# A four-block kernel on one core: the last block's two batch streams put half a period apart, its output projection and expert sums moved between engines

## The reference, cut to what matters

```python
x  = _layernorm(x_in)
n1 = _layernorm(x, ln1_w, ln1_b)
rw = _gating(n1, smha_sim, smha_gates)             # (1024, 8)
q = einsum('btc,ech,bte->bth', n1, q_proj, rw)     # k and v alike, 8 experts
attn = softmax(causal(q @ k.T * scale)) @ v        # (1024, 128)
attn_out = einsum('bth,ehc,bte->btc', attn, o_proj, rw)
hs = x + attn_out
n2 = _layernorm(hs, ln2_w, ln2_b)
rw2 = _gating(n2, moe_sim, moe_gates)
inter = gelu(einsum('btc,eci->btei', n2, w1))      # 8 experts
out = hs + einsum('btei,eic,bte->btc', inter, w2, rw2)
result = x_in + _layernorm(out)
```

## Time and profile before

| what | value |
|---|---|
| median of 3 runs | 3173.81 us (3173.39 to 3175.27) |
| the profiled execution, its own time | 3170.2 us |
| its span, first to last instruction | 3168.4 us |
| busy PE, PEld, DVE | 76%, 53%, 73% of the span |
| busy ACT, POOL | 53%, 40% of the span |
| mean granted TensorE clock | 0.866 |

### The profile page before, as it was taken

The page is one execution under the profiler, slowest core; times in us unless marked ns, Lnnn a source line. Parts: engine busy times, 40 slices in busy tenths (PEclk is TensorE's granted clock), DMA queues, the critical chain, the costliest instruction groups (busy, mean ns, idle before and its releaser), DMA issues.

```text
span 3168.4 us, 41094 instructions
## 1 busy us (share of the span) xinstructions
PE 2407.0 (76%) x14962; PEld 1690.2 (53%) x14962; DVE 2311.8 (73%) x4141; ACT 1678.5 (53%) x2552; POOL 1263.5 (40%) x1203
## 2 busy tenths in 40 slices
PE   3114776667676696899999999999999388667867
PEld 1002444344344564577777777776777366245635
DVE  3994798699599612688878878887888533874386
ACT  4223663665376242678777877787778124022402
POOL 0341143144124200365766576667667540114011
PEclk8556878888788898799999999999999789788978
DMA  3000000000000000100000100010000100000000
GB/s 99 0 0 0 0 1 1 1 1 1 1 1 1 1 1 14 41 21 21 24 21 21 28 21 21 24 29 21 21 21 1 40 1 1 0 14 1 1 0 14
DMA packets 32026, 41.96 MB, mean 13 GB/s; under 512 B 8897, under 2 KB 18130, under 8 KB 31442
## 3 DMA queue, kind: packets, MB, share of 16 engines
q1 hardware_dynamic: 31826, 39.34, 4.6%
HBM read 12.05 MB, written 2.10 MB: 4 GB/s over the span
## 4 chain that ended last, share of the span: by engine, by line
PE 46%; DVE 20%; issue 18%; POOL 11%; ACT 4%; SPq 1%; DMA 1%; POOLq 0%; DVEq 0%; ACTq 0%
PE ps L954 10%; PE ps L932 6%; PE ps L943 6%; POOL MA L379 5%; PE ps L710 3%; DVE MA L1090 3%; DVE MA L1410 3%; PE ps L914 2%; DVE lnb L265 2%; PE ps L1724 2%; PE ps L645 2%; PE ps L1711 2%; PE ps L647 1%; PE ps L646 1%; PE ps L1648 1%
## 5 line engine op out<-in xcount | busy, mean ns | idle before, releaser
L1090 DVE TENSOR_REDUCE MA<-ps 128x1 f32<-128x1024 f32 x512 | 623.1, 1220 | 190.4 <-PE ps L932 177.6
L379 POOL TENSOR_TENSOR MA<-MA,BIG 128x1024 f32<-128x1024 f32 x120 | 280.1, 2355 | 624.3 <-DVE BIG L350 624.3
L954 PE MATMUL ps<-MA,WB 128*64 128x128 f32 x4096 | 504.5, 277 | 0.0
L954 PEld LDWEIGHTS ps<-MA,WB 128*64 128x64 f32 x4096 | 442.8, 137 | 88.4 <-issue 87.4
L344 DVE TENSOR_TENSOR_SCAN BIG<-BIG 128x1024 f32<-128x1024 f32 x128 | 346.8, 2748 | 0.0
L932 PE MATMUL ps<-BIG 96*128 96x512 f16 x1024 | 312.6, 387 | 13.3 <-DMA BIG<-WB 4.9
L632 ACT ACTIVATE HR<-ps,b 128x512 f32<-128x512 f32 x288 | 191.5, 686 | 244.0 <-PE ps L647 243.0
L710 PEld LDWEIGHTS ps<-WB,HR 128*128 128x128 f32 x2304 | 305.8, 209 | 25.0 <-issue 8.7
L710 PE MATMUL ps<-WB,HR 128*128 128x128 f32 x2304 | 312.8, 294 | 0.0
L1017 ACT ACTIVATE WB<-ps,MA 128x1024 f32<-128x1024 f32 x206 | 229.5, 1114 | 149.3 <-DVE MA L1090 147.5
L497 PE MATMUL ps<-bc,sel 96*128 96x512 bf16 x256 | 108.2, 520 | 249.1 <-DVE BIG L350 190.7
(11 more groups left out here) (286 smaller groups left out, 5133.2 us busy)
## 6 DMA issues: line engine op xcount, KB each, us to landing
BIG<-BIG SPq DMA_DIRECT2D x192, 64.0 KB, 2.0
BIG<-WB SPq DMA_DIRECT2D x192, 64.0 KB, 2.0
WB<-w_dram SPq DMA_DIRECT2D x1, 2304.0 KB, 14.6
X<-x_dram SPq DMA_DIRECT2D x4, 512.0 KB, 12.5
HR<-w_dram SPq DMA_DIRECT2D x1, 2048.0 KB, 9.3
out_dram<-X SPq DMA_DIRECT2D x4, 512.0 KB, 3.2
WB<-wqkv_dram SPq DMA_DIRECT2D x1, 1536.0 KB, 6.1
WB<-w_dram SPq DMA_DIRECT2D x2, 512.0 KB, 8.2
```

Source lines behind the costliest of these rows:

```text
L379: e.tensor_tensor(yy[:, c, :], yy[:, c, :], db[n % 2][c], ALU.add).then_inc(*p_my.up(b, n, c))
L954: x = e.matmul(bank[6][64 * pp:64 * pp + 64, 0:128], V[(4 * b + g) % 2][:, k, 64 * pp:64 * pp + 64], DT[n % 2][:, 128 * k:128 * k + 128], ...
L1090: e.tensor_reduce(L_of(n)[:, c:c + 1], ps[s][:, :], AX, ALU.max, negate=True).then_inc(*v_amx.up(n, s))
```

## The change

The planned times get the stream in them: `d_at(k, r, t)` is `D_PERIOD * r + D_SHIFT * k + t` with a period of 193.0 and a shift of 96.0, so in each engine's order stream 1 stands half a period behind stream 0. The weight preparation becomes a generator that is merged with the two streams. The output projection treats each half of the rows and each expert by itself: POOL scales the attention rows (`n1`) by the expert's weight, PE transposes them, ACT copies them, and PE multiplies by that expert's matrix and sums the eight experts in PSUM (`B[h]`, a bank for each half); DVE adds each bank into `hs` once. In the expert phase DVE's four weigh-and-add operations become one 128x512 multiplication into `s_sc`, and POOL adds the result into `hs`. `affine` and the gate get further `yield`s. The removed transposes are those of `turn(r, 1)`.

```diff
-        D_PERIOD, D_EXPERT = 177.2, 3.15
-        D_LN = [(0, 3), (5, 8), (125.4, 128.4), (171.2, 174.2)]
-        D_TR = [11, 110, 131.4]
-        D_GATE = [(13, 16, 19, 21), (131.4, 134.4, 137.4, 139.4)]
+        D_PERIOD, D_EXPERT, D_SHIFT = 193.0, 3.15, 96.0
+        D_LN = [(0, 3), (5, 8), (139.5, 142.5), (187.5, 190.5)]
+        D_TR = [11, 110, 145.5]
+        D_GATE = [(13, 16, 19, 22), (145.5, 148.5, 151.5, 154.5)]
         D_ATT = [76.4 + 3.5 * i + 0.1 * i * (i - 1) for i in range(9)]
-        D_OUT, D_MOE = 111, 142.4
+        D_OUT, D_STEP, D_MOE, D_MSTEP = 111, 1.6, 157, 1.75
-        def d_at(r, t):
-            return D_PERIOD * r + t
+        def d_at(k, r, t):
+            return D_PERIOD * r + D_SHIFT * k + t
-        def d_scaled(r, q):
+        def d_scaled(k, r, q, more=0.0):
+            if q >= 16:
+                return d_at(k, r, D_OUT + D_STEP * (q - 16) - 1.5 + more)
...
         def experts_act(e):
-            e.wait_ge(phase, 8)
+            yield 0.3
...
+            yield 8.5
             e.wait_ge(s_wq, 16)
...
         def experts_dve(e):
-            e.wait_ge(phase, 8)
+            yield 0.2
...
             for a in range(3):
+                yield 13.2 + 3.5 * a
...
...
-                for j in range(8):
-                    yield d_at(r, D_OUT + 1.8 * (j + 1))
-                    e.wait_ge(*t_dom[k].at(r, j))
-                    for x in range(8):
-                        i = e.scalar_tensor_tensor(out=hs[:, j, :], in0=(S0, S1)[j % 2][:, 128 * x:128 * x + 128],
-                                                   scalar=G(6)[:, j, x:x + 1], in1=hs[:, j, :], op0=ALU.mult, op1=ALU.add)
...
+                for h in range(2):
+                    yield d_at(k, r, D_OUT + D_STEP * (8 * h + 9) + 1)
+                    e.wait_ge(*t_dom[k].at(r, 8 * h + 7))
+                    e.tensor_tensor(hs[:, 4 * h:4 * h + 4, :], hs[:, 4 * h:4 * h + 4, :],
+                                    B[h].rearrange("p (j c) -> p j c", c=128), ALU.add).then_inc(*v_dom[k].up(r, h))
...
-                    for j in range(4 * (x // 8), 4 * (x // 8) + 4):
-                        i = e.scalar_tensor_tensor(out=hs[:, j, :], in0=B[2 + x % 2][:, 128 * (j % 4):128 * (j % 4) + 128],
-                                                   scalar=G(6)[:, j, x % 8:x % 8 + 1], in1=hs[:, j, :], op0=ALU.mult,
-                                                   op1=ALU.add)
-                    i.then_inc(*v_dm[k].up(r, x))
+                    e.tensor_tensor(s_sc[k][x % 2].rearrange("p (j c) -> p j c", c=128),
+                                    B[2 + x % 2].rearrange("p (j c) -> p j c", c=128),
+                                    G(6)[:, 4 * h:4 * h + 4, x % 8:x % 8 + 1].to_broadcast([128, 4, 128]), ALU.mult).then_inc(
+                                    *v_dm[k].up(r, x))
...
-                    for q in range(16):
-                        h, x = q // 8, q % 8
-                        yield d_scaled(r, q)
+                    for q in range(32):
+                        h, x = q // 8 % 2, q % 8
+                        yield d_scaled(k, r, q)
...
+                for x in range(16):
+                    yield d_at(k, r, D_MOE + D_MSTEP * (x + 2) + 0.5)
+                    e.wait_ge(*v_dm[k].at(r, x))
+                    h = x // 8
+                    if x % 8:
+                        e.wait_ge(*p_dm[k].at(r, x - 1))
+                    e.tensor_tensor(s_hs[k][:, 4 * h:4 * h + 4, :], s_hs[k][:, 4 * h:4 * h + 4, :],
+                                    s_sc[k][x % 2].rearrange("p (j c) -> p j c", c=128), ALU.add).then_inc(*p_dm[k].up(r, x))
...
-                turned(r, 1)
+                for q in range(16, 32):
+                    yield d_scaled(k, r, q, 1.5)
...
+                    e.activation(s_so[k][q % 2], B[2 + q % 2], ACT.Copy, scale=1.0).then_inc(*a_dhi[k].up(r, q))
...
-                turn(r, 1)
-                for j in range(8):
-                    for h in range(2):
...
-                        i = e.matmul((S0, S1)[j % 2][:, 512 * h:512 * h + 512], xT[k][:, 128 * j:128 * j + 128],
-                                     flat(wo3[:, 4 * h:4 * h + 4, :]), start=True, stop=True)
+                for q in range(16, 33):
+                    if q < 32:
+                        yield d_scaled(k, r, q, 1.5)
+                        e.wait_ge(*p_dsc[k].at(r, q))
...
+                        for j in range(4):
+                            i = e.transpose(B[2 + q % 2][:, 128 * j:128 * j + 128], s_sc[k][q % 2][:, 128 * j:128 * j + 128],
+                                            ident[:, :])
+                        i.then_inc(*t_dst[k].up(r, q))
+                    if q > 16:
+                        y = q - 17
+                        h, x = y // 8, y % 8
+                        yield d_scaled(k, r, q, 2.0)
+                        e.wait_ge(*a_dhi[k].at(r, q - 1))
...
+                        for j in range(4):
+                            c = slice(128 * j, 128 * j + 128)
+                            i = e.matmul(B[h][:, c], s_so[k][y % 2][:, c], wo3[:, x, :], start=x == j == 0, stop=x == 7,
+                                         skip_group_check=True)
+                        i.then_inc(*t_dom[k].up(r, y))
...
-            experts_dve(e)
-            weave(soft_dve(e, 0), soft_dve(e, 1))
+            e.wait_ge(phase, 8)
+            weave(experts_dve(e), soft_dve(e, 0), soft_dve(e, 1))
```

More of the change, by code:

```diff
@@ L1243, in program @@
                 for k in range(2)]
+        s_so = [[big[4 + k][:, 512 * i:512 * i + 512] for i in range(2)] for k in range(2)]
         s_g = [big[7][:, 512 * k:512 * k + 512].rearrange("p (j n) -> p j n", j=8) for k in range(2)]
@@ L1288, in experts_pool @@
         def experts_pool(e):
-            e.wait_ge(phase, 8)
+            yield 6.0
             e.wait_ge(*a_dsp.at("sq"))
@@ L1336, in gating @@
                 top2(e, s_g[k], gidx[k], G(0), G(1), G(4), G(2), G(3)).then_inc(*dve_own.up())
+                ready = dve_own.now()
+                yield d_at(k, r, times[2] + 1.5)
                 e.tensor_scalar(G(7)[:, :, 4:5], G(1)[:, :, 0:1], 0.0, None, ALU.is_le)
                 e.tensor_scalar(G(7)[:, :, 5:6], G(1)[:, :, 0:1], 0.0, None, ALU.max)
-                e.wait_ge(*dve_own.now())
+                e.wait_ge(*ready)
                 e.tensor_tensor(G(2), G(2), G(3), ALU.add).then_inc(*dve_own.up())
@@ L1348, in gating @@
                     *v_dgt[k].up(r, w, "pre"))
-                yield d_at(r, times[3])
+                yield d_at(k, r, times[3])
                 e.wait_ge(*a_dtr[k].at(r, w, "exp"))
@@ L1373, in soft_dve @@
                     e.wait_ge(*t_dtr[k].at(r - 1, 2, 1))
-                affine(r, 1)
+                yield from affine(r, 1)
                 yield from gating(r, 0, D_GATE[0])
                 for q in range(16):
-                    yield d_scaled(r, q)
+                    yield d_scaled(k, r, q)
                     e.wait_ge(*a_dhi[k].at(r, q))
@@ L1419, in soft_dve @@
+                yield d_at(k, r, D_LN[2][0])
+                stats(e, s, hst, {0: v_dom[k].at(r, 0), 4: v_dom[k].at(r, 1)}).then_inc(*v_dln[k].up(r, 2, "stats"))
+                yield d_at(k, r, D_LN[2][1])
                 e.wait_ge(*p_dln[k].at(r, 2, "rstd"))
-                affine(r, 2)
+                yield from affine(r, 2)
                 yield from gating(r, 2, D_GATE[1])
                 for x in range(16):
-                    yield d_at(r, D_MOE + 1.6 * (x + 2))
+                    yield d_at(k, r, D_MOE + D_MSTEP * (x + 2))
@@ L1700, in soft_pe @@
+                yield d_at(k, r, D_TR[2])
                 turn(r, 2)
[L1701 removed]
+                yield d_at(k, r, D_GATE[1][2])
                 logits(r, 2)
@@ L1766, in _ @@
             e.drain().then_inc(phase, 1)
-            experts_act(e)
-            weave(soft_act(e, 0), soft_act(e, 1))
+            e.wait_ge(phase, 8)
+            weave(experts_act(e), soft_act(e, 0), soft_act(e, 1))
         @block.vector
@@ L1786, in _ @@
             e.drain().then_inc(phase, 1)
-            experts_pool(e)
-            weave(soft_pool(e, 0), soft_pool(e, 1))
+            e.wait_ge(phase, 8)
+            weave(experts_pool(e), soft_pool(e, 0), soft_pool(e, 1))
         @block.sync
```

178 lines of the change are left out of this document (86 added, 92 removed).

## The result

The changed kernel takes 3213.51 us (3213.22 to 3218.76, four runs), the kernel before 3173.6 beside it. The ratio is 1.0129, with an interval of 1.0111 to 1.0146: 40 us slower. The forecast was 3135, faster; the range ended at 3180.

A forecast was written before the change was run, and what follows sets the result against it. No engine bounds the whole stage; each phase has its own limit, and PE idles in norms. Lone start 87, three half periods of 147 and lone end 101 make 629 for 667.6, so 3135 us; range 3080 to 3180.

The forecast's parts named there:

- H = 112.6 + 34.5 = 147: Length in us of one half period of the last stage with both streams: PE work 112.6 plus waits 34.5.
- mixed half period: One of three half periods of the last stage in which both streams run, forecast at 147 us each.
- the two lone parts: Start and end of the last stage, where one stream runs alone: 87 and 101 us, sure to some 8 together.
- the 629: Forecast length in us of the last stage, 87 + 3 × 147 + 101, against 667.6 before.
- Lone start: Stream 0 alone at the stage's start: norms, gate, projection and five attention units, 87 us.
- Segments: Four stretches of a mixed half period, by stream 0's planned time 0, 24, 76, 88, 96: 38, 79, 22 and 8 us.
- Rival 1: In mixed half periods PE is nearly full, hiding the other stream's DVE and POOL: 127 us each, 3075 total; chance 0.20.
- Rival 2: POOL operations awaiting DVE hold up the other stream's scalings: half period 171 us, kernel slower at 3207; chance 0.12.
- Rival 3: ACT stands as long again at each table change, 11 us more a half period: 3168 us, about unchanged; chance 0.06.
- Rival 4: POOL's scalings slow DVE's norms, adding 5 us a half period (152): 3150 us, within the forecast; chance 0.14.

The follow-up runs named there:

- in step: The changed kernel with D_SHIFT 0 instead of 96.0, so both streams run in lockstep with the new operations: 3153.4 us, ratio to before 0.9927.
- the idle products: Unread 512-column PE products added to the changed kernel ahead of scores of units 5 to 7: 3228.88 us; to its D_SHIFT 0 version in the norms: 3156.66 us.

## Why the prediction was wrong

**The step that failed** is "H = 112.6 + 34.5 = 147". The two terms were right: 112.7 of work and 32 to 35 of waits. The sum was not, since a mixed half period held 20 to 23 us more, work at low clock and gaps, for which it had no term. Three times 20 is 60, and the two lone parts were 12.4 + 4.0 = 16 over. With these the 629 become 705; measured were 706.

The sign of this omission matters. The kernel before has the same kind of loss, 79.2 in the stage, and it was compared by its measured length, in which that loss is contained. The model of the kernel after was built from full-clock durations and waits alone. Had I put before's loss per half period, 79.2/4 = 20, on each mixed half period and once on the two lone parts together, the sum would have been some 629 + 4 × 20 = 709, and the forecast slower. That it would have come so near is luck, since nothing says that the loss must be the same at another order. I had the earlier trace rows with clocks of 0.55 and 0.50 in the norms, and the last sentence of the prediction named the clock in mixed stretches as a way to be wrong, without a price.

**Why other grew to 101.9** is shown in part. The rows show waits of several us followed by work at the lower level (3.78 for 1.72 in the scores, 0.43 for 0.21 in the projection). A shift turns a few long waits in stretches that have little work anyway into many in front of dense work. PE's busy time times (1 − granted clock), summed over windows of 4 us, gives an estimate of 55 us lost at low clock in the kernel after, 40 before and 30 in step, but only 37 at a shift of 6. The estimate leans on modelled ends of matmuls and on where the window borders fall; the split between clock and unnamed gaps is not settled. At a shift of 6 it would leave the clock 7 of the 46 us that the stage lost, so there the waits and unnamed gaps are most of the loss. Nor did the idle products settle it.

**By the parts of the prediction.** Lone start, 87 against 99.4 by its stretches: statistics to turn 19.3 for 15.8, turn to the first scaled transposes 15.0 for 14.5, projection 45.3 for 40.5, attention to the other stream's statistics 19.8 for 16.5. The first is a queue again: the second norms stand on DVE behind a step of the preparation (L1283) that waits 4.99 us for a power on POOL. Segments: 38, 79, 22 and 8 against 41.1, 90.7, 21.6 and 11.5. Table loads: 25 forecast, 25 found. An addition from PSUM was priced at 0.69 us, the multiplication of that shape (L1438) took 0.69, and the 512-wide addition into `hs` (L1421) 0.68.

**The rivals.**
- *Rival 1*, PE nearly full: no. PE was busy 133 of 165.
- *Rival 2*, POOL's queue: its time, 3207, is close to what came, but not by its mechanism. It wanted 24 us of unpriced waits per batch. All waits of PE for POOL's scalings were 33.1 in four batches, some of them priced, and moving the scalings ahead gained 12. It has a sibling that I didn't name, DVE's queue: scores waiting for an exponential that waits for a maximum behind the other stream's norms. PE's waits for the exponential (L1552) are 33.7 us, where they were 0.7 before; 4.5 of them went with the table loads, so not all are DVE's.
- *Rival 3*, table changes at double price: no. The rows of the kernel after show a load 0.01 after the activation before it and the next activation 0.02 after the load:

```profile
2910.96 0.60 ACT L1579 ACTIVATE HR<-ps 128x512 f32<-128x512 f32 x1 [1.44 <-PE ps L1738]
2911.57 1.28 ACT L1552 ACT_TABLE_LOAD   x1
2912.87 0.47 ACT L1552 ACTIVATE WB<-ps,BIG 128x256 f32<-128x256 f32 x1
```

 All 25 loads together were worth 7 to 8 us, of the 32 that they last. The Trainium skill, "ScalarE: Activation LUTs", section What ACT_TABLE_LOAD costs, adds a drain of 1380 ns to the 1283 of the load. The load agrees with 1.28, and the drain does not show in these rows.
- *Rival 4*, POOL slowing DVE: not seen as a cost. The norms into `MA` (L265) took 353 ns in the mean, less than the 436 before.

**Was it one cause?** The runs show that distance between the streams costs, at 6, 28 and 96 of plan, and with the old operations at 88.6, and that two single couplings are worth 12 and 7 to 8 us that add. They don't show one cause for the remaining 35 to 40. The lone parts, DVE's queue and the low clock all bear on it, and at different shifts in different shares. DVE's queue was not moved by itself, so that stays open.

## What to carry to other kernels

When two streams share in-order engines, price a stagger against the same operations in step, not against the old kernel. Here that would have asked for 148.7 us a half period and shown that the new operations alone win 0.7%.

A sum of work and waits lacks what the same profile loses beyond them. Make the sum for the kernel before first, and carry what is left over into the forecast. Split a change that reorders and also replaces operations, and run the halves apart: two signs can hide in one number.

## What the runs showed of the hardware that was not expected

- TensorE fell to the lower level of its clock in a stretch in which it was busy 11 of 15 us (granted clock 0.51, 2781 to 2796), after short waits. Behind one wait of 5.38 us the transposes and products took about twice as long (1.12 for 0.60, a pitch of 0.43 for 0.21).
- Table loads that alternate with activations every few us, 25 in the stage, cost 7 to 8 us in all of the 32 that they last. The stretch that held them most densely took 21.5 us with them and 16.6 without, and the next stretch took back 3.7 of the difference.
